# The Nystrom gate and the context's side of the next attention in one stage, in a two-layer transformer kernel on one core

## What is computed

```python
# L1_attn (Nystrom), its last lines
enc = xg[0] + dense
A_raw = jax.ops.segment_sum(adj_vals * data[adj_rows, adj_cols], adj_rows, num_segments=n)
alpha = jax.nn.softmax(A_raw)
value = dense @ wv_w + wv_b
xl = alpha[:, None] * value
wei = jax.nn.sigmoid(-xl); sw = wei * wei
xo = xl * 2 * sw + 2 * enc * (1 - sw)
x = _layernorm(x + xo)
# L1_xattn: 16 heads of 64, context of 77 rows
q = (x @ Wq); k = (ctx @ Wk); v = (ctx @ Wv)
probs = softmax(q k^T + bias + mask); x = _layernorm(x + (probs @ v) @ Wo)
```

## Time and profile before

| | |
|---|---|
| median of 3 runs | 2516.03 us (2514.41 to 2516.48) |
| profiled execution, its own time | 2517.56 us |
| its span in the profile | 2515.8 us |
| busy: TensorE, VectorE, ScalarE, GpSimd | 2298.0, 1523.7, 1103.0, 1073.9 us |
| `stage_gate`, from VectorE's first difference | 1971.25 us |
| `stage_ctx`, TensorE's first product | 2005.18 us |
| scores of query tile 0, TensorE | 2028.22 us |

### The profile page before, as it was taken

One profiled execution on the slowest core, in us unless ns is written; L12 is line 12 of the kernel. 1 busy time (PEld: TensorE's weight loads), 2 busy tenths in 40 slices (PEclk: granted clock), 3 DMA queues, 4 the chain that ended last, 5 costly groups with the idle time before them and its releaser, 6 DMA issues.

```text
span 2515.8 us, 34568 instructions
## 1 busy us (share of the span) xinstructions
PE 2298.0 (91%) x12918; PEld 1438.5 (57%) x12918; DVE 1523.7 (61%) x2281; ACT 1103.0 (44%) x2349; POOL 1073.9 (43%) x785
## 2 busy tenths in 40 slices
PE   6999999879988999999899998799899589989998
PEld 3333443357754555555555554588656467768887
DVE  6778678357745666663766666432444556656556
ACT  1667567623323444441344444133322457743233
POOL 2556547424444788873668888033401122100000
PEclk7899999999999999999999999899999699989999
DMA  6354433232110111112011111255210141010001
GB/s 127 117 95 94 82 62 69 65 77 40 1 18 1 14 14 15 10 34 35 2 14 15 14 10 18 69 134 134 31 55 22 51 117 51 1 59 17 1 1 34
DMA packets 138067, 114.50 MB, mean 46 GB/s; under 512 B 74823, under 2 KB 115253, under 8 KB 137517
## 3 DMA queue, kind: packets, MB, share of 16 engines
q1 hardware_dynamic: 100749, 111.36, 16.5%
q0 software_dynamic: 36864, 0.15, 4.3%
q10 hardware_dynamic: 288, 0.79, 0.2%
HBM read 86.26 MB, written 13.40 MB: 40 GB/s over the span
## 4 chain that ended last, share of the span: by engine, by line
PE 69%; DVE 12%; DMA 9%; ACT 3%; issue 3%; POOL 2%; SPq 2%; DVEq 0%; POOLq 0%; ACTq 0%
PE PS L120 66%; DMA adj<-e_EE,e_IX 7%; DVE c_MX L1784 2%; SPq L146 2%; DVE g_SS L124 1%; PE PS L1189 1%; DVE c_WS L124 1%; ACT a_P L839 1%; POOL c_AC L124 1%; DVE a_MX L733 1%; DVE g_st L1274 1%; PE PS L352 1%; DMA a_KS<-a_KL 1%; DVE X L396 1%; DMA a_r<-a_RQ 0%
## 5 line engine op out<-in xcount | busy, mean ns | idle before, releaser
L345 POOL DMA_INDIRECT adj<-e_EE,e_IX x256 | 414.4, 1619 | 460.9 <-DMA adj<-e_EE,e_IX 348.8
L124 POOL TENSOR_TENSOR c_AC<-c_AC,c_P 128x1024 f32<-128x1024 f32 x150 | 379.5, 2530 | 90.4 <-DVE c_AC L124 83.3
L1784 DVE TENSOR_REDUCE c_MX<-PS 128x2 f32<-128x1024 f32 x256 | 312.7, 1221 | 170.5 <-PE PS L120 170.5
L1881 ACT ACTIVATE c_P<-PS 128x1024 f32<-128x1024 f32 x256 | 250.9, 1026 | 237.9 <-PE PS L120 230.0
L733 DVE TENSOR_REDUCE a_MX<-PS 128x2 f32<-128x1024 f32 x256 | 303.4, 1219 | 59.2 <-PE PS L120 57.9
L839 ACT ACTIVATE a_P<-PS 128x512 f32<-128x512 f32 x512 | 270.5, 601 | 91.1 <-PE PS L120 90.2
L120 PE MATMUL PS<-c_P,c_VV 128*64 128x512 f32 x1024 | 247.7, 605 | 0.0
L129 POOL TENSOR_SCALAR e_EQ<-e_KR,e_KC 128x128 bf16<-128x128 f32 x256 | 162.8, 636 | 159.3 <-DMA e_KR<-adj_key 122.9
L120 PE MATMUL PS<-a_QS,a_KS 64*128 64x512 f32 x512 | 195.0, 463 | 16.2 <-ACT a_P L839 8.5
L120 PE MATMUL PS<-a_KS,a_QS 48*128 48x512 f32 x512 | 170.8, 475 | 12.0 <-DVE a_MX L733 4.9
L120 PEld LDWEIGHTS PS<-a_QS,a_KS 64*128 64x128 f32 x512 | 84.4, 190 | 169.0 <-ACT a_P L839 96.6
(11 more groups left out here) (499 smaller groups left out, 4620.3 us busy)
## 6 DMA issues: line engine op xcount, KB each, us to landing
e_KR<-adj_key SPq DMA_DIRECT2D x64, 256.0 KB, 3.7
f_W<-in_L_ffn_w SPq DMA_DIRECT2D x16, 1024.0 KB, 7.9
c_RB<-c_r SPq DMA_DIRECT2D x60, 128.0 KB, 2.9
g_FB<-in_fside_1x16xSxS SPq DMA_DIRECT2D x8, 616.0 KB, 8.0
a_QS<-a_QH SPq DMA_DIRECT2D x32, 128.0 KB, 3.9
adj<-e_zt SPq DMA_DIRECT2D x16, 256.0 KB, 4.2
adj<-e_EE,e_IX POOLq DMA_INDIRECT x256, 3.2
d_AJ<-adj SPq DMA_DIRECT2D x8, 512.0 KB, 7.6
```

What stands on the lines that cost most here:

```text
L124: return v.e.tensor_tensor(o, a, b, op)
L345: g.e.indirect_dma_start(self.adj, bass.IndirectOffsetOnAxis(ap=self.IXE[:, k:k + 1], axis=0), self.EE[:, k:k + 1], None, compute_op=ALU.a ...
L1784: v.e.reduce_max(MX[:, w % 2, :, qt, kh], bank(0, 2).rearrange("p (h n) -> p h n", h=2), AX, negate=True).then_inc(*smax_dve.up())
L1881: s.e.activation(PB[t % NP][:, :, :].rearrange("p h n -> p (h n)"), bank(2 + 2 * (t % 2), 2), ACT.Exp, scale=0.125).then_inc(*st_act.up())
```

## The change

`stage_gate` is gone as a stage. Its work is now a class `Gate`, whose methods are called from `stage_ctx`, in the same block, without a barrier. The second layer's schedule is a new one: the 19 steps of the gate alternate with the 20 jobs of the context's side. Then come one root and reciprocal for all sixteen tiles ("roots"), and tiles 0 to 3 ("front": normalised by ScalarE, transposed into bank 7, copied by ScalarE). Tiles 4 to 15 are normalised by VectorE in iterations 0 to 5 of the attention's loop ("lnorm", two in each) and transposed and copied in iterations 1 to 6 ("lturn", two in each, all through bank 7). GpSimd's first g_BM waits until all tiles are mixed. The tiles of `stage_ctx` are laid over those of `stage_d` that are free, at given places; the sigmoid's tile is K.LS, the bias of the norm is part of `stt`.

```diff
+            side = list(context())
+            for n in range(19):
+                yield "gate", n
+                yield side.pop(0)
+            yield from side
+            yield "roots",
+            for t in range(4):
+                yield "front", t
         for i in range(16 + lag):
...
             else:
+                for t in range(2 * i + 2, 2 * i + 4) if 1 <= i < 7 else ():
+                    yield "lturn", t
                 if i < 16:
                     yield "exp", i
                 if 1 <= i < 17:
                     yield "soft", i - 1
+                for t in range(2 * i + 4, 2 * i + 6) if i < 6 else ():
+                    yield "lnorm", t
                 if 2 <= i < 18:
                     yield "out", i - 2
...
+                if not first:
+                    pe.wait_ge(gate.xt_act, i + 1)
...
+            elif kind in ("front", "lturn"):
+                t, = a
+                bank_free(7)
+                gate.tensor(t, 7)
+                free[7] = [(gate.xt_act, t + 1)]
...
+            elif kind == "front":
+                gate.norm_act(*a)
+                gate.copy_act(*a, 7)
+            elif kind == "lturn":
+                gate.copy_act(*a, 7)
...
+                g.wait_ge(gate.mix_dve, 16)
...
+    def roots_dve(self):
+        v, SA = self.K.dve, self.K.SA
+        v.wait_ge(self.sd_act, 1)
+        v.step(v.e.reciprocal(SA[:, :, 8], SA[:, :, 9]))
+        sst(v, self.NM, SA[:, 0:4, 6], -1.0, SA[:, 0:4, 8], ALU.mult, ALU.mult).then_inc(*self.rs_dve.up())
+
+    def norm_act(self, t):
+        s, X = self.K.act, self.K.X
+        s.wait_ge(self.rs_dve, 1)
+        s.e.activation(X[:, t, :], X[:, t, :], ACT.Identity, bias=self.NM[:, t:t + 1],
+                       scale=self.K.SA[:, t, 8:9]).then_inc(*self.x_act.up())
+
+    def copy_act(self, t, bk):
+        s = self.K.act
+        s.wait_ge(self.xt_pe, t + 1)
+        s.e.copy(self.K.XT[:, :, t * 128:t * 128 + 128], halves(self.K.bank(bk)[:, 0:256])).then_inc(*self.xt_act.up())
```

More of the change, by code:

```diff
@@ L992, in load, with stage_ctx @@
             dma(sp, W, A[name].rearrange("(c p) n -> p c n", p=128)).then_inc(*landed.up())
[L995 removed]
+def stage_ctx(K, block, pre, scale, W, gate=None):
     A, X, XT, CT, bank = K.A, K.X, K.XT, K.CT, K.bank
@@ L1001, in stage_ctx, with sb @@
     E = K.edges
+    first = gate is None
     c = ExitStack()
-    sb = K.sb
+    def sb(c, name, shape, area=None):
+        if first:
+            return K.sb(c, name, shape)
+        area = area or ROOM
+        size = 4 * math.prod(shape[1:])
+        area[1] += -(-size // 32) * 32
+        return K.over(name, area[0], area[1] - -(-size // 32) * 32, shape, F32)
+    FRONT, LATER, ROOM = ["d_WA", 0], ["d_EN", 0], ["d_AJ", 0]
     if first:
@@ L1052, in schedule @@
                 yield "m", k, q
+    def schedule():
+        if first:
+            yield from context()
+        else:
+            side = list(context())
[6 more added lines that the diff above has]
+                yield "front", t
         for i in range(16 + lag):
@@ L1238, in vector @@
                                 bank(bk)[:, 0:154 * n].rearrange("p (a n) -> p a n", n=154)).then_inc(*kp_dve.up())
+            elif kind == "gate":
+                gate.vector(*a)
+            elif kind == "roots":
+                gate.roots_dve()
+            elif kind == "lnorm":
+                gate.norm_dve(*a)
             elif kind == "wt" and a[0] % 2 == 0:
@@ L1381, in gpsimd @@
             kind, *a = job
-            if kind == "out" and first:
+            if kind == "gate":
+                gate.gpsimd(*a)
+            elif kind == "out" and first:
                 E.send(g, 3)
@@ L2964, in stage_d @@
     c2.close()
[L2965 to L3049, removed]
-            s.e.activation(SA[:, tiles, 9], SA[:, tiles, 7], ACT.Sqrt, bias=K.epsc[:, 0:1]).then_inc(*sd_act.up())
-            if k == 0:
-                s.wait_ge(rs_dve, 1)
-                for i in range(8):
-                    s.e.activation(X[:, i, :], X[:, i, :], ACT.Identity, bias=NM[:, i:i + 1],
-                                   scale=SA[:, i, 8:9]).then_inc(*x_act.up())
-                    if i:
-                        turned(i - 1)
-                turned(7)
-        for i in range(8, 16, 2):
-            turned(i)
-    def turned(i):
-        s.wait_ge(xt_pe, i + 1)
-        s.e.copy(XT[:, :, i * 128:i * 128 + 128], halves(bank(2 + i % 4)[:, 0:256])).then_inc(*xt_act.up())
-    def gpsimd(_):
-        K.behind(g)
-        for i in range(1, 16, 2):
-            g.wait_ge(sq_act, i + 1)
-            g.wait_ge(dif_dve, i + 1)
-            g.step(tt(g, EN[:, i, :], EN[:, i, :], SG[:, i % 4, :], ALU.mult), mul_pool)
-    def sync(_):
-        K.behind(sp)
-    K.run(block, tensor, vector, scalar, gpsimd, sync)
-    c.close()
```

95 lines of the change are left out of this document (82 added, 13 removed).

## The result

The changed kernel takes 2511.5 us, median of 20 runs, the kernel before 2519.32 us on the same chip, median of 20. The ratio is 0.9969 with a 95% interval from 0.9957 to 0.998: 7.8 us faster. Timed once more on another chip, beside the versions at the end of the experiments, it gave 2511.93 against 2517.32 us, a ratio of 0.9982, interval 0.9966 to 0.9998. So the gain is some 5 to 8 us, where 1.6 were forecast, and about 0.2 to 0.3%; the first comparison lies beyond the bound of 0.2% under which I had put the most chance. In the two profiles the stretch from VectorE's first difference of the gate to the end of the span takes 544.5 us before and 536.3 after, 8.2 us less.

What follows compares the result with a forecast made beforehand. VectorE's queue was taken as the limit until tile 0's scores, TensorE's from there. The terms summed as 8.1 - 2.3 - 4.2 = 1.6 us gained, from a median of 2516.03 to 2514.4 us, range 2508 to 2520.

Steps and rivals of the forecast that it cites:

- step 1: Merged gate and context: VectorE's list sets the time, 4.2 us lost waiting for tile 2's square; last m copy at 2011.55.
- step 2: Ahead of the fronts: GpSimd's second bias sum locks out VectorE's small product into stt, costing 2.1 us.
- rival A: At the roots: the small product slips between or before GpSimd's two bias sums, 2.1 us come back, 2512.3; chance 0.16.
- Step 3: Four front tiles go singly through one bank, 1.64 us each; tile 0's scores start at 2020.1, gain so far 8.1 us.
- Step 4: Tile 0's scores: TensorE starts cold, 4.6 us at half clock, losing 2.3 us.
- Step 5: Attention loop, iterations 2 to 6: transposes through bank 7 add 1.15 us each, 0.84 after the slack, 4.2 us in all.
- Rival B: Attention loop: the transposes are hidden and only some 0 to 1 us is paid, 2510.2; chance 0.12.
- Rival C: Tile 0's scores: the clock is up, since the merged stretch gives TensorE work all along, 2512.1; chance 0.08.
- Rival D: First loop iterations: the clock stays down one iteration longer, costing 11 us, 2525.4; chance 0.08.

Runs made afterwards that it cites:

- experiments 1 and 4: On the changed kernel: 1, roots' reciprocal done three times, turn of tile 14 at 217.36 us; 4, context's jobs begin behind gate step 3, scores at +44.39.
- experiment 7: Changed kernel plus 28 unread TensorE products, 16 while it waits for the roots, 4 behind each of three fronts; turn of tile 14 at 212.29 us.
- Version 2: Changed kernel with two loop banks, four pipelined front banks, GpSimd's first sum behind the small product, plus unread TensorE products during the roots' wait and behind fronts; 2499.27 us.
- versions 1 and 2: The first is the changed kernel with two loop banks, four pipelined front banks and GpSimd's first sum behind the small product, 2502.54 us; the second adds unread products, 2499.27.

## Why the prediction was right or wrong

The mechanisms were named rightly, but step 1 was mis-sized and the wait of step 2 did not come, and both erred to the same side. Against the sum of 1.6 us the marks give 7.9.

**Step 1, 3.2 us too dear.** TensorE's start was put at 1971.2, level with VectorE, with a remark that it could be 0.8 us earlier. It started 1.3 us before VectorE:

```profile
1968.25 6.95 PE L121 MATMUL PS<-CT,g_WV 128*128 128x154 f32 x32 [2.08 <-issue]
```

The second copy of values came 5.93 us behind that, not 5.65, and so the multiply of tile 2 came at +6.06 and not +7.05: 1.0 us. From there to the last m copy I counted 33.25 us; it took 31.04. The fifteen copies cost 7.7 us of VectorE's list and not 9.02: the 9.02 of the earlier trace rows is their busy time in a stretch where each stood alone, while in a full list the next instruction starts some 0.1 us before such a row ends. Four mixes met GpSimd (0.95 us) and not six as before, 1.0 us less; and there was no wait at the first "u" (0.3, less 0.4 of small things). The form of the step, one queue summed up, was right: VectorE has hardly any other wait until the roots.

**Step 2, nearly the right price for something that did not happen.** Met, the lock costs 1.9 to 2.0 us, as experiments 1 and 4 show (2.10 and 2.16 us for a product that takes 0.17 alone), against 2.1. The order of events was rival A's: I had the product 0.5 us behind the second sum's start, it came 0.1 us ahead of it. I had written that my count errs by more than that, and still gave A only 0.16 and put the full 2.1 into the sum. Both hang on VectorE's one list, the sum on the mix of tile 15, so that an error of step 1 moves them together and only the distance from that mix to the product counted. I had 3.2 us for it; it is 2.7 (2004.13 to 2006.85), mostly since three m copies in a full list took 0.48 us each and not 0.60. The second sum starts 2.8 us behind the mix. So rival A was decided by the same fault as step 1's copies, and a distance taken from pitches would have shown it to be even odds at least.

The Trainium skill, SBUF — State Buffer, section "Who interferes with whom", says that the order of issue decides who blocks. The rows agree: the mix at 1988.24, 0.08 us behind GpSimd's multiplication, took 0.95 us, and a GpSimd multiplication that came while VectorE was at work with two operands took 1.09 and not 0.73 to 0.75:

```profile
1979.93 0.41 DVE L125 TENSOR_TENSOR d_EN<-d_EN,LS 128x256 f32<-128x256 f32 x1
1980.18 1.09 POOL L125 TENSOR_TENSOR d_EN<-d_EN,LS 128x256 f32<-128x256 f32 x1 [2.58 <-DVE d_EN L135]
1980.27 0.41 DVE L135 SCALAR_TENSOR_TENSOR X<-d_EN,X 128x256 f32<-128x256 f32 x1
```

**Step 3** put a front's period at 1.64 us; it is 1.71, and the fronts cost 6.4 us where 6.0 stood. The gain at the scores was 13.1 and not 8.1 by 1.0 (start), 2.2 (the list), 2.2 (the wait for the lock, 2.1, and 0.1 in pitches), less 0.4 here.

**Step 4** held: 2.3 us forecast, 2.1 between the traces (15.90 less 13.82), 2.2 by experiment 7. Behind the first turn the kernel before had a low clock too: the interval to the second turn has a mean clock of 0.81 in both traces, as these windows show, of before and of the changed kernel:

```profile
2042.04:2055.79 13.75, 13.45 (x51) 9.04 (x51) 6.49 (x8) 8.01 (x42) 2.58 (x1) 0.81 0.20 47
```

```profile
2029.29:2043.84 14.55, 14.09 (x54) 9.66 (x55) 7.67 (x11) 10.65 (x56) 2.58 (x1) 0.81 0.08 23
```

It grew from 13.75 to 14.55 us; two banks give back 0.55 of that (14.00), so that some 0.25 us at most were missing from the step. The 1.0 us that experiment 7 saves there, at 0.87, is for the larger part a gain over the kernel before and not a loss by the change.

**Step 5** named the right cause, the second pair's wait for bank 7, and the right price of it: 1.12 us in the trace, 1.15 in the forecast. The slack was too small. I took the 0.31 us that the trace shows ahead of the turn. But "out" takes 4.80 us to the turn there and 4.32 now that nothing is waited for, so the slack is 0.48, and an iteration loses 0.6 us instead of 0.84 (the first of the five 0.8); over the five intervals to the sixth turn 3.2 us instead of 4.2.

**What else.** Rival B is refuted: the loop does not hide the pairs. Rival C is refuted, the clock was 0.50. Rival D is refuted: from the second turn on the periods are regular. The last interval of the stage, 12.04 us before and 10.63 after, goes with the clock. A window from the turn of tile 14 to the next one, of the kernel before:

```profile
2193.73:2205.77 12.04, 9.14 (x38) 7.52 (x36) 2.73 (x5) 4.99 (x26) 0.00 (x0) 0.72 0.00 0
```

The changed kernel:

```profile
2184.15:2194.78 10.63, 7.73 (x38) 6.53 (x37) 2.73 (x5) 4.99 (x26) 0.00 (x0) 0.84 0.00 0
```

Version 2:

```profile
2178.53:2187.73 9.20, 6.30 (x37) 5.49 (x36) 2.73 (x5) 4.99 (x26) 0.00 (x0) 1.00 0.00 0
```

In all fourteen profiles it takes 9.2 us at a mean clock of 1.00, 10.6 to 10.7 at 0.84, and 11.9 to 12.3 at 0.71 or 0.72, with the busy times of VectorE and ScalarE the same to 0.02 us. So these 1.4 us are the clock's; nothing in the forecast bears on them. Why a kernel has one or another clock there was not tried. Why D0 moves by 13 us between executions is open as well.

That the forecast of 2514.4 lies only 2.9 us from the median of 2511.5 is partly luck: it was counted from the 2516.03 of three runs, and the kernel before has a median of 2519.32 over twenty. The gain, 1.6 us against 7.8, was off by much more.

With the marks' 7.9 us in place of 1.6 the working would have given 2508.1, 0.3% below, and "faster" most of the chance. The range, 2508 to 2520, holds the measured 2511.5; taken by the ratio against the 2516.03 of the runs shown, the kernel would stand at 2508.2, at the range's low end.

## What to carry to other kernels

Two stages with opposite limits, one bound by VectorE with TensorE idle, the next the other way round, are worth laying side by side job by job; taking the barrier away and leaving the lists in order gave 1 us of the 8. Whatever is squeezed into a loop of a full TensorE should have a bank for each piece: with one bank the twelve tiles' transposes cost 3.2 us, with two 0.2. And where a tiny instruction stands on the critical path and a long GpSimd instruction with SBUF inputs may be under way beside it, make GpSimd wait for it: it cost nothing that shows here, and otherwise a tenth of a microsecond somewhere ahead decides over two.

## What the runs showed of the hardware

Between two GpSimd instructions 0.08 us apart a VectorE instruction that arrives just then passes, and an instruction of 0.17 us that comes 0.5 us into the second one ends only with it and takes 2.10 us. TensorE's clock is worth buying: sixteen products with no use, put into a wait that was there anyway, kept it at 1.00 until the first turn and brought 3.0 us at tile 14 between versions 1 and 2. And in a row without a wait behind it a matmul group's pitch is about 0.16 us less than its duration (4.32 for 4.48), so the idle time that a bracket shows after such a row understates the slack by as much.
